# The order of K's and Q's products, stores and loads in an attention kernel, and the place of a phase's probabilities

## The reference, cut to what matters

```python
def attention(x, ctx, energy):                       # 16 sequences; x 224 x 512, ctx 750 x 512, all float32
    Q = layernorm(x) @ Wq + bq                       # 16 heads of 32
    K = ctx @ Wk + bk;  V = ctx @ Wv + bv
    s = Q @ K.T / sqrt(32) * gate                    # gate: 0.1 or 1 by key, from energy
    x = x + tanh(g0) * (softmax(s) @ V @ Wo + bo)
    return x + tanh(g1) * moe(layernorm(x))          # 2 of 16 experts and 2 shared ones
```

## Time and profile before

| | |
|---|---|
| median of 3 runs | 2111.77 us (2110.38 to 2112.2) |
| the profiled execution's own time | 2115.32 us |
| its span, first to last instruction | 2113.6 us |
| mean granted TensorE clock | 0.963 |
| TensorE busy | 92% of the span |
| period of a sequence in the attention | some 88 us, fifteen with a next sequence to prepare |

### The profile page before, as it was taken

One profiled execution on the slowest core, in us unless ns is written; L12 is line 12 of the kernel. 1 busy time (PEld: TensorE's weight loads), 2 busy tenths in 40 slices (PEclk: granted clock), 3 DMA queues, 4 the chain that ended last, 5 costly groups with the idle time before them and its releaser, 6 DMA issues. The chain is left out here.

```text
span 2113.6 us, 41157 instructions
## 1 busy us (share of the span) xinstructions
PE 1939.9 (92%) x12484; PEld 1508.4 (71%) x12485; DVE 1132.4 (54%) x1791; ACT 759.8 (36%) x1503; POOL 1246.8 (59%) x1422
## 2 busy tenths in 40 slices
PE   1899999999999999999999999998617999999999
PEld 1777878778787787877878778785315666678887
DVE  3465655655556565565655656555293333345565
ACT  1144454444444444454444444443221222210000
POOL 3267776777767777677776777766454333232331
PEclk9999999999999999999999999997558999999999
DMA  5746548365483754836548375470264444444553
GB/s 162 186 115 179 154 129 242 101 184 147 133 241 100 187 149 131 239 104 185 151 130 236 101 190 150 129 213 21 81 265 135 143 147 149 139 128 136 174 150 111
DMA packets 167257, 324.80 MB, mean 154 GB/s; under 512 B 20135, under 2 KB 69287, under 8 KB 166839
## 3 DMA queue, kind: packets, MB, share of 16 engines
q1 hardware_dynamic: 154084, 289.83, 48.2%
q0 software_dynamic: 10880, 33.56, 5.8%
q10 hardware_dynamic: 2256, 0.94, 0.2%
HBM read 211.42 MB, written 112.39 MB: 153 GB/s over the span
## 5 line engine op out<-in xcount | busy, mean ns | idle before, releaser
L804 DVE TENSOR_REDUCE neg_max<-score 112x1 f32<-112x750 f32 x512 | 480.4, 938 | 567.6 <-PE score L1065 566.4
L603 ACT ACTIVATE probs_t<-st 125x448 f32<-125x448 f32 x768 | 413.9, 542 | 521.1 <-PE st L1091 518.4
L460 POOL TENSOR_TENSOR acc<-acc,probs_t 125x448 f32<-125x448 f32 x256 | 307.7, 1202 | 66.9 <-ACT probs_t L603 65.5
L1091 PE MATMUL st<-q_stack,k_stack 98*125 98x224 f32 x1536 | 335.2, 301 | 5.6 <-ACT probs_t L603 3.0
L1091 PEld LDWEIGHTS st<-q_stack,k_stack 98*125 98x125 f32 x1536 | 268.6, 192 | 61.0 <-issue 28.0
L462 POOL TENSOR_TENSOR acc<-acc,probs_t 125x448 f32<-125x448 f32 x256 | 294.6, 1151 | 20.1
L1065 PE MATMUL score<-k_stack,q_stack 96*112 96x512 f32 (+1 forms) x1024 | 285.5, 360 | 19.5 <-DVE neg_max L804 10.2
L452 POOL TENSOR_TENSOR acc<-probs_t 125x448 f32<-125x448 f32 x128 | 146.1, 1143 | 170.1 <-PE pv L1117 150.1
L1065 PEld LDWEIGHTS score<-k_stack,q_stack 96*112 96x112 f32 x1024 | 160.4, 179 | 74.0 <-issue 49.2
L1108 PE MATMUL pv<-probs_t,v_sb 125*32 125x224 f32 x3072 | 191.9, 369 | 6.6 <-DVE out_t L827 5.9
L1029 PE MATMUL proj<-ctx_hi,wk_hi 128*128 128x376 f32 (+1 forms) x512 | 184.0, 359 | 9.4 <-POOL ctx_lo L415 9.4
(11 more groups left out here) (198 smaller groups left out, 3173.8 us busy)
## 6 DMA issues: line engine op xcount, KB each, us to landing
k_stack<-k_parts SPq DMA_DIRECT2D x192, 375.0 KB, 6.3
ctx_raw<-in_ctx_t SPq DMA_DIRECT2D x64, 375.0 KB, 9.9
k_parts<-k_hi SPq DMA_DIRECT2D x64, 375.0 KB, 6.7
k_parts<-k_lo SPq DMA_DIRECT2D x64, 375.0 KB, 7.2
y_slots<-y_sb SPq DMA_DIRECT2D x72, 256.0 KB, 2.9
q_stack<-q_parts SPq DMA_DIRECT2D x64, 224.0 KB, 4.0
x_in<-in_x SPq DMA_DIRECT2D x16, 448.0 KB, 9.0
q_parts<-q_hi SPq DMA_DIRECT2D x64, 112.0 KB
```

Source lines behind the costliest of these rows:

```text
L460: nc.gpsimd.tensor_tensor(both, both, tiles(c, p, pair, 0), ALU.add).then_inc(half_added, 1)
L603: act.activation(probs_t[0:KW, (c * PHASES + p) % 2, u % HC, :], st[u % 2][0:KW, 0:2 * L], ACT.Exp)\
L804: nc.vector.tensor_reduce(neg_max[:, h // HC % 2, h % HC, t:t + 1], score[0:QW, 0:S], axis=AX.X, op=ALU.max, negate=True).then_inc(maxed, 1)
L1091: ins = nc.tensor.matmul(st[u % 2][0:KW, k * L:(k + 1) * L], k_stack[0:SHIFTED, h, kt * KW:(kt + 1) * KW], q_stack[0:SHIFTED, h, :], start ...
```

## The change

In the attention alone: (1) `K0b` goes ahead of `Q0` in `BODY`, on TensorE, and in the copies on the three other engines; (2) SP stores K before Q for stack 0, and `load_stack` loads K's three parts before Q's two, for every stack; (3) the first phase's `attend` of every stack follows the next score instead of standing ahead of it.

```diff
-BODY = (... "K0a", "Q0", "K0b", "SH2", "Q1", ...
+BODY = (... "K0a", "K0b", "Q0", "SH2", "Q1", ...
@@ SP, load_stack
                     sp.wait_ge(st_done, tiles_done)
+                sp.wait_ge(k_stored[c % 2], k_landed)
+                for row, part in enumerate((0, 0, 1)):
+                    sp.dma_start(k_stack[...], k_dram[...]).then_inc(stacked[c], 16)
                 sp.wait_ge(q_stored, q_landed)
                 for rows, w in (((0, 2 * DH), (0, 2)), ((2 * DH, ROWS), (0, 1))):
                     sp.dma_start(q_stack[...], q_dram[...]).then_inc(stacked[c], 16)
-                sp.wait_ge(k_stored[c % 2], k_landed)
-                for row, part in enumerate((0, 0, 1)):
-                    sp.dma_start(k_stack[...], k_dram[...]).then_inc(stacked[c], 16)
@@ SP, batch
+                    store_k(n, 0)
                     store_q(n, 0, b)
-                    store_k(n, 0)
                     load_stack(n, 0, ticks(b, 1, 0))
@@ POOL, batch
+                    key_low(n, "K0a")
                 add_pair(b, 1, 1, 0)
+                    key_low(n, "K0b")
                 add_pair(b, 1, 1, 1)
-                    key_low(n, "K0a")
                 add_pair(b, 1, 2, 0)
-                    key_low(n, "K0b")
@@ ScalarE, stack 1, behind the exponential of tick u
-                    if not last and u == 6:
-                        query_high(n, 0, b)
+                    if not last and u == 4:
+                        key_high(n, "K0a", b)
                     if u == 7:
                         shift_high(b, 2, b)
-                    if not last and u == 7:
-                        key_high(n, "K0a", b)
+                        if not last:
+                            key_high(n, "K0b", b)
                     if u == 8:
+                        if not last:
+                            query_high(n, 0, b)
                         place_shift(b, 2, b)
-                    if not first and u in (8, 9):       (normalize x_res)
+                    if not first and u in (9, 10):      (normalize x_res)
-                    if not last and u == 10:
-                        key_high(n, "K0b", b)
@@ VectorE, batch
                 next_maximum(b, 11, 0)
+                    gate_keys(n, "K0a", b)
                 next_maximum(b, 11, 1)
                 normalize_output(b, 0, base, None if first else b)
                 next_maximum(b, 12, 0)
-                    gate_keys(n, "K0a", b)
+                    gate_keys(n, "K0b", b)
                 next_maximum(b, 12, 1)
                 shift_low(b, 2, b)
+                next_maximum(b, 13, 0)
                     query_low(n, 0, b)
-                next_maximum(b, 13, 0)
-                    gate_keys(n, "K0b", b)
                 next_maximum(b, 13, 1)
@@ TensorE, stack 0 (stacks 2 and 3 alike)
                 score_columns(b, 0, 7)
-                attend(b, 0, 0)
                 project_out(b - 1, 0, b, (2, 3))
                 next_scores(b, 8, 1)
+                attend(b, 0, 0)
@@ TensorE, stack 1 (the order before | the order after)
 next_scores 11,0              | next_scores 11,0
 Q0 steps 0-2                  | K0b chunk 0
 score_columns 4               | score_columns 4
 Q0 step 3                     | K0b chunk 1
 next_scores 11,1              | next_scores 11,1
 Q0 step 4                     | K0b chunk 2
 score_columns 5               | score_columns 5
 Q0 steps 5-7                  | K0b chunk 3
 score_columns 6               | score_columns 6
                               | Q0 steps 0-1
 next_scores 12,0              | next_scores 12,0
 K0b chunk 0                   | Q0 steps 2-3
 score_columns 7               | score_columns 7
 attend(b, 1, 0)               |
 K0b chunk 1                   | Q0 step 4
 next_scores 12,1              | next_scores 12,1
 K0b chunk 2                   | attend(b, 1, 0)
 turn_shift, score_columns 8   | turn_shift, score_columns 8
 K0b chunk 3, Q1 steps 0-1     | Q0 steps 5-7
 score_columns 9               | score_columns 9
 next_scores 13,0              | next_scores 13,0
 Q1 steps 2-4                  | Q1 steps 0-1
 score_columns 10, attend 1,1  | score_columns 10, attend 1,1
 Q1 step 5                     | Q1 steps 2-3
 next_scores 13,1              | next_scores 13,1
                               | Q1 step 4
 score_columns 11              | score_columns 11
 Q1 steps 6-7, K1a chunks 0-1  | Q1 steps 5-7, K1a chunks 0-1
```

More of the change, by code:

```diff
@@ L38 @@
 LOWEST = -3.4028234e38
-BODY = ("V4", "V5", "O0", "SH1", "O1", "XT0", "XT1", "K0a", "Q0", "K0b", "SH2", "Q1", "K1a",
+BODY = ("V4", "V5", "O0", "SH1", "O1", "XT0", "XT1", "K0a", "K0b", "Q0", "SH2", "Q1", "K1a",
         "K1b", "K2a", "K2b", "K3a", "SH3", "K3b", "YT0", "YT1", "LG", "V0", "V1", "SH0", "V2", "V3")
@@ L290, in load_stack @@
                     sp.wait_ge(st_done, tiles_done)
+                sp.wait_ge(k_stored[c % 2], k_landed)
+                for row, part in enumerate((0, 0, 1)):
+                    sp.dma_start(k_stack[row * DH:(row + 1) * DH, c * HC:(c + 1) * HC, :].bitcast(F32),
+                                 k_dram[bass.ds(n, 1), c, part, :, :, :].rearrange("a j p s -> (a p) j s"))\
+                        .then_inc(stacked[c], 16)
                 sp.wait_ge(q_stored, q_landed)
@@ L669, in batch @@
                         copy_turned(b, f"XT{u}", u)
-                    if not last and u == 6:
-                        query_high(n, 0, b)
+                    if not last and u == 4:
+                        key_high(n, "K0a", b)
                     if u == 7:
                         shift_high(b, 2, b)
-                    if not last and u == 7:
-                        key_high(n, "K0a", b)
+                        if not last:
+                            key_high(n, "K0b", b)
                     if u == 8:
+                        if not last:
+                            query_high(n, 0, b)
                         place_shift(b, 2, b)
-                    if not first and u in (8, 9):
-                        if u == 8:
+                    if not first and u in (9, 10):
+                        if u == 9:
                             act.wait_ge(x1_stored, b * 16)
-                        normalize(x_res, u - 8, xn2_ready, 2 * b if last else 2 * b + 1)
-                    if not last and u == 10:
-                        key_high(n, "K0b", b)
+                        normalize(x_res, u - 9, xn2_ready, 2 * b if last else 2 * b + 1)
                 for u in range(TICKS):
@@ L1228, in batch @@
                 if not last:
-                    project_q(0, b, (0, 3))
+                    project_k(n, "K0b", b, (0, 1))
                 score_columns(b, 1, 4)
                 if not last:
-                    project_q(0, b, (3, 4))
+                    project_k(n, "K0b", b, (1, 2))
                 next_scores(b, 11, 1)
                 if not last:
-                    project_q(0, b, (4, 5))
+                    project_k(n, "K0b", b, (2, 3))
                 score_columns(b, 1, 5)
                 if not last:
-                    project_q(0, b, (5, 8))
+                    project_k(n, "K0b", b, (3, 4))
                 score_columns(b, 1, 6)
+                if not last:
+                    project_q(0, b, (0, 2))
                 next_scores(b, 12, 0)
                 if not last:
-                    project_k(n, "K0b", b, (0, 1))
+                    project_q(0, b, (2, 4))
                 score_columns(b, 1, 7)
+                if not last:
+                    project_q(0, b, (4, 5))
+                next_scores(b, 12, 1)
                 attend(b, 1, 0)
-                if not last:
-                    project_k(n, "K0b", b, (1, 2))
-                next_scores(b, 12, 1)
-                if not last:
-                    project_k(n, "K0b", b, (2, 3))
                 turn_shift(b, 2, b)
@@ L1252, in batch @@
                 if not last:
-                    project_k(n, "K0b", b, (3, 4))
-                    project_q(1, b, (0, 2))
+                    project_q(0, b, (5, 8))
                 score_columns(b, 1, 9)
@@ L1257, in batch @@
                 if not last:
-                    project_q(1, b, (2, 5))
+                    project_q(1, b, (0, 2))
                 score_columns(b, 1, 10)
@@ L1261, in batch @@
                 if not last:
-                    project_q(1, b, (5, 6))
+                    project_q(1, b, (2, 4))
                 next_scores(b, 13, 1)
+                if not last:
+                    project_q(1, b, (4, 5))
                 score_columns(b, 1, 11)
                 if not last:
-                    project_q(1, b, (6, 8))
+                    project_q(1, b, (5, 8))
                     project_k(n, "K1a", b, (0, 2))
@@ L1301, in batch @@
                 score_columns(b, 2, 7)
-                attend(b, 2, 0)
                 if not last:
@@ L1305, in batch @@
                 next_scores(b, 16, 1)
+                attend(b, 2, 0)
                 score_columns(b, 2, 8)
@@ L1360, in batch @@
```

(2 more changed lines are left out.)

10 lines of the change are left out of this document (3 added, 7 removed).

## The result

The kernel after takes **2160.15 us** (median of 6 runs, 2150.18 to 2178.59) against 2111.07 of the kernel before, run beside it (6 runs, 2108.03 to 2112.68): a ratio of 1.0244, 95% interval 1.0199 to 1.0290. It is slower by 2.4% (the medians differ by 49 us), where the forecast was 2113 and the range ended at 2128. The profiled execution took 2163.77 us with a span of 2162.1 and a mean granted clock of 0.956 (0.963 before).

A forecast was written before the change was run, and what follows sets the result against it. TensorE, busy 92% of the span, was taken as the bound. Per-sequence terms summed to +0.15 us, fifteen times +2.3; less the last sequence's 0.8, +1.5 on the median of 2111.8: 2113 us, range 2096 to 2128.

The forecast's parts named there:

- Part 1: Stack 1, K0b ahead of Q0: bank wait goes, some 0.4 us wait at score (12,1), tick (2,3) reached 0.7 us sooner.
- Part 2: Q's store issued 1.75 us later, so ScalarE is late and tick (2,3) lags 0.5 us per sequence; upper bound 1.5.
- Part 3: Load order: stack 0's wait for K's rows goes, -0.77 us, 0.07 back; `x_res` in the tail costs 0.05 per sequence.
- Part 4: `attend` behind the next score: maxima bind, +0.15 us each in stacks 0 and 2, 0 in stack 3, per sequence.
- the landing of Q's store: Four stores taken to land in 7.9 us as before, so the later issue moves the landing to about 1028.2.
- The last sequence: With no next one to prepare, it gains some 0.8 us, as `attend` no longer waits for the normalization.
- A: The forecast: Q's late store gives back what the two removed waits gave; 2113 us, own range 2108 to 2118; chance 0.36.
- B: Faster: Q's store or low part is done sooner, ScalarE isn't late at tick (2,3); 2095, half gives 2104; chance 0.34.
- C: Slower by POOL: Q's loads behind K's delay `x_res` by two issues and more data; 2129 us; chance 0.17.
- D: Slower by Q's loads, now last of stack 0: 1.3 us wait instead of 0.07, +18, likelier half, 2122; chance 0.1.
- E: Slower: waits don't change as said, for example maxima bind in all four stacks, 0.4 us each; 2133; chance 0.03.

The follow-up runs named there:

- e9_qfirst: Kernel after, with Q's loads ahead of K's again in every stack and K's store still first: 2145.64 us, ratio 1.0173.
- e2_loads: Kernel before, with only K's three loads put ahead of Q's two in `load_stack`: 2149.66 us, ratio 1.0165.
- e14_after_all: Kernel after plus Q's HBM buffer by part, stack 1's loads held until stack 3's shift rows landed, `x_res` reloaded ahead of stack 2's loads: 2090.18 us.
- e15_before_all: Kernel before with the same three edits as `e14_after_all`: 2103.03 us, ratio 0.9973.
- e5_wide: Kernel after, with Q's HBM buffer laid out by part, so a store is 128 rows in one block and Q's loads are three: 2134.09 us.
- e12_wide_gate: `e5_wide` plus a wait on SP holding stack 1's loads until stack 3's shift rows have landed: 2104.01 us, ratio 0.9948.

## Why the prediction was wrong

**Part 1 was right.** Measured from the stack-0 sum, it had score (12,1) at 6.9 and score (13,0) at 9.9; they came at 6.79 and 9.88. The wait of 0.4 us at score (12,1) is not in the profile's list of waits, but the rows show it: the Q step ahead of that score starts 0.67 us before it, where a step takes some 0.38, and the score starts at 687.34, right behind the maximum that ends at 687.28. The wait on the bank went, and the lead of 0.7 us at tick (2,3) was there (20.25 against 20.96).

**Part 2 had the mechanism and missed a size.** "The new issue is at 1020.3, 1.75 us later": it was 1.69. "Landing to about 1028.2" took the store's 7.9 us over unchanged; it was 9.03. With that the lag is 1.59 us and not 0.5. The part had 1.5 as its upper bound, but for the wrong reason: it named K's stores ahead in the queue. `e9_qfirst` shows it is K's *loads* beside the store; without them its landing took 7.9 us, and its stack 1 lost 0.58 us, near the lag that the part forecast. The loads were in part 3, four microseconds earlier than before. That part asked what Q's store would do to them, and not what they would do to the store, which was still running.

**Part 3 was right in its sum.** The wait of the earlier trace rows for K's stack is gone, and stack 2 takes 19.76 us in a typical sequence where it took 20.46 in the mean: -0.70 for the -0.77 + 0.07 forecast. That it came out to the digit is luck: the typical sequence before took 20.25, and the mean holds some with slower loads. Q's last loads cost 1.6 us in two waits, and x_res nothing, in the kernel after; `e2_loads` shows that both would have in the old order.

**Part 4 was small and a little too high.** Stack 0 is 0.05 longer, not 0.15. In stack 2 at most 0.1 can be its own (19.77 us in `e14_after_all`, 19.70 in the typical sequence of `e15_before_all`), and stack 3 shows nothing. Alone, the edit costs 0.34%, nearly all of it in stack 1, for which the part had no price.

So a typical sequence costs 1.0 us more and not 0.15. The step that failed there is one term, the landing of Q's store: 7.9 us in the sum, 9.03 measured. That alone would have made it some 2127 us, at the end of the range. The last sequence gave more than the 0.8 us put down for it: from its stack-0 sum to its last sum it took 51.30 us instead of 54.95, at a mean granted clock of 0.69 instead of 0.60.

**What was missing altogether** is the larger part, some 32 of 47 us: what a new wait of 1.5 to 3.1 us brings about later in the same sequence. The prediction put two things at nothing. One is a fall of the granted clock, some 20 us by the windows: the kernel before shows none in the fifteen sequences that prepare a next one, but it shows several in its last one, the first behind a wait of 1.42 us, and that was the place to read what a new wait may bring. The other is the shift rows, 14 us of waits, whose two small DMAs on ScalarE's queue it followed only as far as stack 2's (part 2). Those of stack 3 had no wait of note before and were not followed at all. Their cover was the distance to stack 1's K loads, 3 us in the kernel before (1044.13, against this row), and in the kernel after 1.4 us at best:

```profile
1041.09 1.30 ACTq L618 DMA_DIRECT2D q_stack<-shift_rows  x2
```

**The rivals.** A's mechanism decided, at three times its size and with a tail. B (no late ScalarE) is what `e5_wide` made true in stack 1, where it gave 0.88 us. C and D did not decide in the kernel after, and each did in another run. E was a seventh of the loss by the ratios, a fifth by the stacks of the profiled executions (0.62 of 3.14 us a sequence).

## What to carry to other kernels

When a transfer's landing is a term of the sum, ask what the same change puts beside it: a duration read where the queue was quiet holds only while nothing else is issued. Follow every transfer of the sequence that has a consumer on the bounding engine, those with no wait today among them, and note which ones it must stay ahead of. And when an order looks right and runs slower, price its transfers before giving it up: this one was worth 12.9 us once a layout, one wait and one reload had been put right.

## What had not been expected of the hardware

- A wait of TensorE of 2.06 us, ended at 608.57, was followed by a stretch at half clock while the engine was busy: the windows from 610 to 614 read 0.60, 0.50, 0.50 and 0.69. Such stretches came after some of these waits and not after others: all fifteen sequences wait at tick (2,3), and six have one behind it. Those six waits are of 2.06 to 3.09 us, the nine others of 1.50 to 2.48, so the length alone doesn't decide. What does was not settled.
- A small transfer issued among large ones is late by microseconds: two DMAs of 3.5 KB took 7.4 us from issue until TensorE went on (621.84 to 629.23). With the large loads held back until they had landed, those loads went out 2.7 us after the small ones' issue (1034.76 to 1037.46 in `e12_wide_gate`).
- Q's store moved its bytes in 3.2 us instead of over 6, by the layout of its buffer in HBM.
